# Attention in a two-layer kernel: probabilities normalised and split in SBUF, then turned by DMA transposes instead of TensorE

## The reference, cut to what matters

```python
q = jnp.einsum('bse,ehd->bshd', x, wq)      # k, v likewise; x: (1, 1024, 256)
qn = rms_norm(q, q_scale)                   # kn likewise
scores = jnp.einsum('bqhd,bkhd->bhqk', qn, kn)
attn = jax.nn.softmax(scores, axis=-1)
out = jnp.einsum('bhqk,bkhd->bqhd', attn, v)
return jnp.einsum('bqhd,hde->bqe', out, wo)
```

## Time and profile before

| | us |
|---|---|
| median of 3 runs | 1154.66 (1150.30 to 1156.62) |
| the profiled execution | 1158.08 |
| its span | 1156.4 |
| PE busy | 1055.9 (91%) |
| DVE busy | 799.4 (69%) |
| ACT busy | 623.3 (54%) |
| POOL busy | 433.8 (38%) |

### The profile page before, as it was taken

How to read it: one execution, slowest core, us unless ns; L and a number is a source line. 1 busy time by engine, 2 the same in 40 slices (tenths; PEclk the granted TensorE clock), 3 DMA queues, 4 the chain that set the end, 5 groups by cost and what they waited for, 6 DMA issues and landing times. The chain is left out here.

```text
span 1156.4 us, 20372 instructions
## 1 busy us (share of the span) xinstructions
PE 1055.9 (91%) x7438; PEld 709.4 (61%) x7438; DVE 799.4 (69%) x1413; ACT 623.3 (54%) x1225; POOL 433.8 (38%) x385
## 2 busy tenths in 40 slices
PE   5967989999999999999999999989979679899797
PEld 4455766666666666666666666559525266577444
DVE  4778167777877787778787778835689936563266
ACT  3564166666666666666666666723611047546341
POOL 3313354542544254425452424030085015622263
PEclk7965999999999999999999999999979979899798
DMA  5673111112111212121212110140122057568622
GB/s 174 121 214 115 27 29 37 35 49 60 38 49 35 60 37 58 27 58 37 60 24 60 38 33 10 33 123 2 55 79 108 32 167 229 166 212 266 223 87 87
DMA packets 136152, 97.07 MB, mean 84 GB/s; under 512 B 38724, under 2 KB 129398, under 8 KB 135798
## 3 DMA queue, kind: packets, MB, share of 16 engines
q1 hardware_dynamic: 118550, 72.56, 23.1%
q10 hardware_dynamic: 14432, 14.81, 3.8%
q0 software_dynamic: 3072, 8.39, 2.2%
HBM read 69.32 MB, written 23.79 MB: 81 GB/s over the span
## 5 line engine op out<-in xcount | busy, mean ns | idle before, releaser
L1254 DVE TENSOR_REDUCE a_nmax<-psum 128x1 f32<-128x1024 f32 x128 | 156.4, 1222 | 89.1 <-PE psum L1102 87.5
L1024 POOL TENSOR_TENSOR a_rnorm<-a_ss,a_power 128x8 f32<-128x8 f32 x32 | 57.6, 1801 | 319.2 <-DVE a_ss L1230 319.1
L1260 DVE SCALAR_TENSOR_TENSOR a_pT<-psum,a_pT 128x512 f16<-128x512 f32 x256 | 163.8, 681 | 17.9 <-ACT a_pT L1197 15.9
L1197 ACT ACTIVATE a_pT<-psum 128x512 f16<-128x512 f32 x256 | 139.6, 604 | 13.0 <-PE psum L1113 11.8
L1189 ACT ACTIVATE a_ex<-psum,a_nmax 128x1024 f32<-128x1024 f32 x128 | 142.8, 1116 | 0.3 <-DVE a_nmax L1254 0.2
L1113 PEld LDWEIGHTS psum<-ident,a_ex 128*128 128x128 f32 x1024 | 120.6, 141 | 25.1 <-issue 0.7
L1113 PE MATMUL psum<-ident,a_ex 128*128 128x128 f32 x1024 | 133.4, 274 | 0.0
L1084 PE MATMUL psum<-a_wh,xT_h 128*128 128x128 f16 (+1 forms) x512 | 115.3, 248 | 2.0 <-PEq L2686 2.0
L1085 PE MATMUL psum<-a_wl,xT_h 128*128 128x128 f16 (+1 forms) x512 | 115.3, 248 | 0.0
L1086 PE MATMUL psum<-a_wh,xT_l 128*128 128x128 f16 (+1 forms) x512 | 115.2, 248 | 0.0
L1124 PE MATMUL psum<-a_pT,a_vh 128*128 128x512 f16 x256 | 97.5, 381 | 4.6 <-DVE a_of L944 3.4
(11 more groups left out here) (392 smaller groups left out, 2474.5 us busy)
## 6 DMA issues: line engine op xcount, KB each, us to landing
a_rb<-row_scales SPq DMA_DIRECT2D x32, 256.0 KB
block_outputs<-g_e_ym ACTq DMA_DIRECT2D x16, 512.0 KB, 3.5
split_rest<-a_e_wh SPq DMA_DIRECT2D x15, 384.0 KB, 5.6
wf<-in_L_ffn_W_gate SPq DMA_DIRECT2D x32, 128.0 KB, 2.5
wf<-in_L_ffn_W_up SPq DMA_DIRECT2D x32, 128.0 KB, 2.5
wf<-in_L_ffn_W_down SPq DMA_DIRECT2D x32, 128.0 KB, 2.9
g_rows<-sorted_tokens SPq DMA_DIRECT2D x16, 256.0 KB, 4.5
g_e_raw<-in_L_ffn_wg SPq DMA_DIRECT2D x32, 128.0 KB, 3.2
```

What stands on the lines that cost most here:

```text
L1197: act.activation(pT[g][:, 0, 4 * h:4 * h + 4, (m % 4) * P:(m % 4 + 1) * P], bank_of(r, unit).rearrange("p (k q) -> p k q", k=4), ACT.Copy, ...
L1254: dve.tensor_reduce(nmax[:, k:k + 1], score_banks(m), AX.X, ALU.max, negate=True).then_inc(max_ready, 1)
L1260: dve.scalar_tensor_tensor(low, bank_of(r, unit).rearrange("p (k q) -> p k q", k=4), PROB, high, ALU.mult, ALU.subtract).then_inc(low_done, 1)
```

## The change

After the exponential of a tile, VectorE makes the factor 4096 / sum for its 128 rows (`shares`: a multiply of one column and a reciprocal). ScalarE writes the high half of the whole tile, scaled by that factor, to SBUF (`tile_high`), VectorE the low half (`tile_low`), and SP turns both halves in one DMA transpose of 128 x 2048 float16 (`turn_tile`) into `pT`. There are three buffers of such halves. TensorE's `tile` is gone, and so are the row scales: no store, no load, no multiplication of the outputs, which are now split straight from PSUM with a factor 1/4096. The products with v move one step later (steps 5, 6, 7, 0 and 1 to 4) and have two PSUM banks, the sides' ring has two. TensorE's sides come ahead of the values. SP's store of a chunk of later weights moves one head later, and the halves of `SplitWeights` have one buffer.

```diff
-    VALUES = {4: (0, 0, 0), 5: (0, 0, 1), 6: (0, 0, 2), 7: (0, 0, 3), 0: (1, 1, 0), 1: (1, 1, 1), 2: (1, 1, 2), 3: (1, 1, 3)}
-    VB = 3
+    VALUES = {5: (0, 0, 0), 6: (0, 0, 1), 7: (0, 0, 2), 0: (1, 0, 3), 1: (1, 1, 0), 2: (1, 1, 1), 3: (1, 1, 2), 4: (1, 1, 3)}
+    OUT_AT = {2: 0, 6: 1}
+    VB, PB = 3, 3
...
-    S_BANK, O_BANK, RING = 0, 6, (4, 5, 7)
+    S_BANK, O_BANKS, RING = 0, (7, 6), (4, 5)
...
+        def tile_high(act, t, m):
+
+            i = QT * t + m
+            act.wait_ge(share_ready, i + 1)
+            if i >= PB:
+                act.wait_ge(turned[i % PB], 16 * (i // PB))
+            act.activation(halves[i % PB][:, :, 0, :], ex[m % 2][:, :].rearrange("p (k q) -> p k q", q=P), ACT.Copy,
+                           scale=share[:, m:m + 1]).then_inc(p_high, 1)
+
+        def tile_low(dve, t, m):
+            i = QT * t + m
+            dve.wait_ge(p_high, i + 1)
+            dve.scalar_tensor_tensor(halves[i % PB][:, :, 1, :], ex[m % 2][:, :].rearrange("p (k q) -> p k q", q=P),
+                                     share[:, m:m + 1], halves[i % PB][:, :, 0, :], ALU.mult, ALU.subtract).then_inc(p_low, 1)
+
+        def turn_tile(sp, t, m):
+
+            i, g, cols = QT * t + m, m // 4, slice((m % 4) * P, (m % 4 + 1) * P)
+            wait_low(sp, t, m)
             if t > 0:
-                sp.wait_ge(of_ready, 2 * t + g - 1)
-            sp.dma_start(rb[g][:, :], row_dram[t, g, :].partition_broadcast(P)).then_inc(row_loaded[g], 16)
+                sp.wait_ge(pv_ready, 2 * t + g - 1)
+            sp.dma_start_transpose(pT[g][:, :, :, cols].rearrange("p k a q -> p (k a) q"),
+                                   halves[i % PB][:, :, :, :].rearrange("p k a q -> p (k a q)")).then_inc(turned[i % PB], 16)
...
                 for t in range(H):
+                    turn_tile(sp, t, 0)
                     if t + 3 < H:
                         load(t + 3)
-                    store_scales(t, 0)
+                    turn_tile(sp, t, 1)
+                    if t > 0:
+                        later.store(sp, t - 1)
+                    if 0 < t < later.CHUNKS - 1:
+                        later.load(sp, t + 1)
+                    turn_tile(sp, t, 2)
...
                 def head(t, r):
                     for m in range(QT):
-                        if m < QT - 1:
-                            exps(t, m + 1)
-                        elif coming(t, 1):
-                            exps(t + 1, 0)
-                        for h in range(2):
-                            tile(t, m, h, r)
+                        u, after = (t, m + 1) if m < QT - 1 else (t + 1, 0)
+                        if u < H:
+                            exps(u, after)
                         for unit in sides_at(t, m):
                             side(t, unit, r)
-                        if m % 4 == 0 and not (fixed(t) and t == 0):
-                            high_outputs(act, t - 1, m // 4)
+                        if m in OUT_AT and t > 0:
+                            high_outputs(act, t - 1, OUT_AT[m])
+                        if u < H:
+                            tile_high(act, u, after)
...
+                def shares(t, m):
+                    dve.wait_ge(exp_ready, QT * t + m + 1)
+                    dve.tensor_tensor(part[:, m:m + 1], total[:, m:m + 1], unit_share[:, :], ALU.mult).then_inc(part_ready, 1)
+                    dve.wait_ge(part_ready, QT * t + m + 1)
+                    dve.reciprocal(share[:, m:m + 1], part[:, m:m + 1]).then_inc(share_ready, 1)
 
                 def head(t, r):
-                    past = not (fixed(t) and t == 0)
                     for m in range(QT):
-                        if m % 4 == 0 and past:
-                            finished(dve, t - 1, m // 4)
+                        tile_low(dve, t, m)
+                        if m < QT - 1:
+                            shares(t, m + 1)
+                        elif coming(t, 1):
+                            shares(t + 1, 0)
                         if m < QT - 2:
                             maxima(t, m + 2)
                         elif coming(t, 1):
                             maxima(t + 1, m + 2 - QT)
-                        if m % 4 == 3:
-                            inverse(t, m // 4)
-                        for h in range(2):
-                            tile(t, m, h, r)
```

More of the change, by code:

```diff
@@ L807, in store, with wait_stored @@
     def store(self, sp, k):
-        b = k % 2
         sp.wait_ge(self.ready, k + 1)
[L810 to L814, removed]
+        sp.dma_start(self.rest[:, :, k * self.WIDTH:(k + 1) * self.WIDTH], self.halves[:, :, :]).then_inc(self.stored, 16)
+    def wait_stored(self, engine, chunks):
+        engine.wait_ge(self.stored, 16 * chunks)
 def attention0(nc, env, w):
@@ L856, in has_low @@
     def has_low(unit):
[L857 removed]
+        return unit[2] >= QK
     def lows(some):
@@ L939, in finished, with wait_low @@
[L939 to L944, removed]
+        def wait_low(engine, t, m):
+            engine.wait_ge(p_low, QT * t + m + 1)
+        def tile_high(act, t, m):
[5 more added lines that the diff above has]
+                           scale=share[:, m:m + 1]).then_inc(p_high, 1)
@@ L946, in low_outputs, with wait_turned @@
+        def wait_turned(engine, t, g):
+            for i in range(QT * t + 4 * g, QT * t + 4 * g + 4):
+                engine.wait_ge(turned[i % PB], 16 * (i // PB + 1))
+        def high_outputs(act, t, g):
+            act.wait_ge(pv_ready, 2 * t + g + 1)
+            act.activation(oT_h[:, t, g * HALF:(g + 1) * HALF], psum[:, O_BANKS[g], :], ACT.Copy, scale=1.0 / PROB).then_inc(o_high, 1)
         def low_outputs(dve, t, g):
             dve.wait_ge(o_high, 2 * t + g + 1)
-            low, high = (x[:, bass.ds(t, 1), g * HALF:(g + 1) * HALF].rearrange("p o q -> p (o q)") for x in (oT_l, oT_h))
@@ L949, in low_outputs @@
[L949 to L952 removed]
+            low, high = (x[:, t, g * HALF:(g + 1) * HALF] for x in (oT_l, oT_h))
+            dve.scalar_tensor_tensor(low, psum[:, O_BANKS[g], :], 1.0 / PROB, high, ALU.mult, ALU.subtract).then_inc(o_low, 1)
         def split_stored(engine):
@@ L993, in _ @@
                               .then_inc(wo_loaded, 16)
[L994 to L1001, removed]
-                        load_scales(sp, t, 1)
+                    for m in range(3, QT):
+                        turn_tile(sp, t, m)
                 sp.wait_ge(wo_loaded, 32)
@@ L1033, in _ @@
                     if t + 1 < H:
-                        normalise(t + 1)
+                        for half in range(2):
+                            normalise(t + 1, half)
                     if t + 3 < H:
```

124 lines of the change are left out of this document (42 added, 82 removed).

## The result

The changed kernel took 1113.93 us (median of 4 runs, 1112.24 to 1118.01) beside 1152.6 us for the kernel before (median of 4): a ratio of 0.967, 95% interval 0.963 to 0.971. It is faster by 3.3%; the forecast had said 1168 us, slower. Rival (1), the power that frees the port, had said 1112.

The account below looks back on a forecast made before the run. VectorE was taken to bound a head: 28.9 us own work, 8.3 port waits, 2.4 for ScalarE, 39.6 against 38.2 us. Together +13 us on 1154.7 gave 1168 us; the case's own range 1150 to 1195, overall 1085 to 1200.

Parts of the forecast that it names:

- Rival (1): GpSimd's power frees the port once its eight columns are read: 35.8 us a head, 1112 us; chance 0.24.
- The step that failed: VectorE/GpSimd port: a VectorE operation arriving during a GpSimd power waits for its end, part of 8.3 us a head.
- The other port waits: VectorE waiting for GpSimd's multiply or splits: share 1.35 at tile 3, low 1.4 and share 1.35 at tile 4.
- the walk: Stepping through one head with VectorE as the bound, from the low of tile 7, to sum its port waits: 8.3 us.
- rival (2): VectorE keeps the port from low to share, so only lows wait, 3.3 us: 34.6 us a head, 1096 us; chance 0.14.
- rival (3): The port costs little and TensorE bounds at 31.2 us a head: 1048 us; chance 0.10.
- VectorE's own work: VectorE's operations in one head, summed without any wait: 28.9 us.
- ScalarE's waits: VectorE waiting for ScalarE's high half before tiles 2, 6 and 7: 0.2 + 0.9 + 1.3 = 2.4 us a head.
- some 31.2 a head: TensorE's time alone per head once the probability transposes leave it, small stalls kept; 30.6 us without them.
- SP and the DMA engines: Transposes of 2048 columns: 2.45 us each on SP, 19.6 a head, landing at about 5; covered, taken as nothing.
- rival (4): Transposes become the longest stage; at 5.5 us a tile on SP, 44 us a head, 1242 us; chance 0.10.
- The tail: End of attention: row scale's way through DRAM goes, last transpose's 5 us comes; zero, within 2 us either way.

Follow-up runs that it names:

- e3: Changed kernel with each GpSimd power run twice, one behind the other: 1107.8 us, ratio to the kernel before 0.957.
- e1: Changed kernel with GpSimd's weight splits left out and write-only memsets of about the same length in their place: 1084.4 us (one run).
- e5: Changed kernel with the weight splits left out and two-column memsets in their place, so GpSimd is almost idle there: 1078.3 us (one run).
- e4: Changed kernel with the first multiply of each GpSimd weight split run twice: 1146.2 us, ratio to the kernel before 0.991.
- e12: Changed kernel plus share's product on ScalarE, splits and GpSimd's q/k multiply in halves, high half of tiles 6 and 7 before the sides: 1070.0 us, ratio 0.922.
- e14: Changed kernel plus share's product on ScalarE, GpSimd's split operations and its q/k multiply in halves; high halves stay behind the sides: 1068.3 us, ratio 0.924.
- e2: Changed kernel with the share's one-column product moved from VectorE to ScalarE: 1088.5 us, ratio to the kernel before 0.942.
- e13: Changed kernel with only GpSimd's multiply of q and k by their norms done in two halves: 1130.5 us, ratio to the kernel before 0.977.

## Why the prediction was wrong

- **The step that failed**: "no row shows a VectorE operation that arrives during a power, and by the page that one waits as well, which gives the sum above." showed a power that is held up, and from that it was concluded that it also holds up. It does not: 1.0 + 1.7 + 1.5 = 4.2 us of the 8.3 a head were put on the power (the low of tile 0 and the product behind it, the product at tile 2), and are not there. The Trainium skill (SBUF — State Buffer, "SBUF: two separate sides") says that the first comer keeps the port for its whole instruction; the measurement differs for this one (a low of 1.27 and a product of 0.15 inside a power of 1.64, here and in e3), and agrees for the multiply and the splits (2.62 and 1.42). Rival (1) had named the reason, eight columns in 1.64 us, and got 0.24. That a VectorE operation isn't held is shown; why the power lets it through, and for how long it takes the port itself, is not. Rival (1)'s 1112 beside 1113.9 is partly luck: its 35.8 us a head doesn't follow from its own terms (39.6 - 4.2 = 35.4, measured 35.1), and it counted 13 heads as shorter by 2.4 us or more, of which the first became 2.4 longer. It should still have been the forecast: with two uses of one rule, the one read from rows of large operations, the other from none, the second deserved no more than half.
- **The other port waits** were put at 1.35 + 1.4 + 1.35 = 4.1 us and measured 4.6. The kinds of wait were right: a low behind a GpSimd operation, the next split behind that low, the product behind the split. The places were right only in part. The forecast let the low of tile 3 through and held that of tile 4 for 1.4; measured is 1.34 at tile 3 and nothing at tile 4, and 0.20 and 0.48 at tiles 1 and 5 that the walk didn't have. That the sums are so close is partly luck. e1 and e5 (without splits the multiply's 1.6 us are left) and e4 (7.3 us with more splits) show their cause. The products that wait 1.27 and 1.28 us rule out rival (2), the head of 35.1 us rules out rival (3).
- **VectorE's own work**: 28.9 forecast, 28.9 measured, here and in e5. **ScalarE's waits**: 2.4 forecast before three tiles, 1.6 measured before one, tile 7. So 39.6 - 4.2 + 0.5 - 0.8 = 35.1.
- **TensorE**: 30.6 us and "some 31.2 a head" as a floor; 31.0 and 31.7 in e12. In the changed kernel it idles, as forecast, 2.22 us before the eight transposes of q and k at 434.02. These then take 1.97 us where the eight before them took 1.04: the granted clock is 0.50, the lower level, from 434.00 to 436.10 and 1.00 around 428. TensorE's order of time:

```profile
428.18 1.04 PE L1076 MATMUL psum<-ident,qk 128*128 128x128 f32 x8
...
434.02 1.97 PE L1076 MATMUL psum<-ident,qk 128*128 128x128 f32 x8 [2.22 <-DVE a_qkTl L1226]
```

- **SP and the DMA engines**: 2.45 us and landing 5 forecast, 1.95 and 4.4 measured. Hidden in the heads, as said; rival (4) is out. But the room is smaller than it looked: in e12 and e14 the DMA share is 0.9, and ScalarE waits twice in 70 us for a transpose, 1.6 us in sum, which no steady head of the changed kernel does. So the transposes may stand next behind TensorE.
- **The tail** was put at zero, within 2 us: from the last head's second maximum to the next block 39.6 us before, 39.9 after. The sum was right, though not for the reason given: it holds 10.3 us of TensorE waiting for transposes that stand behind or beside 2 MB of weights, in the place of the waits for the row scales.
- The 3.1 us before the first maximum, the first head's 2.4 us more and the 2.8 us behind attention were not forecast and their causes were not tried.

## What to carry to other kernels

When work is moved onto an engine that shares a port, list every operation of the other engine with its kind and its length, and price only those for which a row shows that they hold a second one up; that an operation can be held up does not show that it holds. A tiny operation with two SBUF inputs between large ones of the neighbour is the first to move to another engine: here eight products of 0.15 us cost 1.85 us a head, more by their waits than by their work. Cutting the neighbour's operations in two as well left 1.6 us of port waits (e14) of the 2.9 that stood without the cut (e2). Port waits depend on phase, so a single cut can lose (e13) where all of them together win (e12, e14).

## What was not expected of the hardware

A GpSimd power of 128x8 waits for a running VectorE low (2.60 in place of 1.64) but lets the operations that come during it by (a low of 1.27, a product of 0.16). A transpose of 128x2048 float16 from SBUF to SBUF holds SP's queue for 1.95 us (median of all 128), and for 4.6 us each behind 2 MB of loads (9.1 for two). ScalarE does a one-column scaling in 0.20 us; moving it there from VectorE, which did it in 0.15, took the ratio to the kernel before from 0.967 to 0.942.
